# A graph network's node stages: the turn of the rows one pipeline step earlier, and another order of copies, roots and transfers

## Chip, cores and metric
The kernel runs on one core of one Trainium2 chip, in one launch. The metric is device time in microseconds (us), from the first to the last instruction with what lies around it. TensorE, VectorE, ScalarE, GpSimd and SyncE are called PE, DVE, ACT, POOL and SP in the profile. Each works through its own list of instructions in order; semaphores make one wait for another.

## What is computed
A two-layer graph transformer on 6250 nodes with 128 features and 100,000 edges, all in float32. Of the reference, what the node stages compute:

```python
h = relu(layernorm(x))                                  # first node stage
for l in range(2):
    k, q, v = (typed_linear(emb, ntype, W[l]) for W in (Wk, Wq, Wv))   # weights by node type (8)
    # per edge: k and v of the source go through a 16x16 matrix per head (8) and relation (8)
    # softmax over the edges of a target node, weighted sum of v: agg
    out = silu(typed_linear(agg, ntype, Wa[l]))
    al = sigmoid(skip[l][ntype])[:, None]
    out = out * al + emb * (1.0 - al)
    emb = (out - mean(out)) / sqrt(var(out) + 1e-5) * g[l] + b[l]
return x + emb @ Wff + bff
```

## The kernel before
Preparation (sort, lists, tables) fills the first 200 us or so. Then node stage 0, edge stage 0, node stage 1, edge stage 1 and node stage 2 follow one another. Each edge stage waits for the node stage ahead of it, and each node stage for the edge stage ahead.

All three node stages are the function `node_stage` with `l` = 0, 1 or 2; `first` is stage 0 and `last` is stage 2. The nodes are sorted by type into `TT` = 56 tiles of 128 rows, so that a tile has one type and one weight matrix; a type's last tile is mostly empty, and rows that stand for no node are not written.

One tile goes through these steps. (1) In stages 1 and 2, GpSimd gathers the sums of the edges (`n_ag`, L1113), TensorE turns them (L1035), ScalarE copies them out (`n_ag_t`, L952), TensorE multiplies by `Wa` (L1042), ScalarE applies silu (L958), and VectorE mixes with the old rows `h` (L838, L843). (2) VectorE takes mean and variance (L852, L856); for each group of four tiles VectorE adds epsilon (L861), ScalarE takes the root (`root`, L963) and VectorE the inverse (L866). Sqrt and silu need different activation tables, so an ACT_TABLE_LOAD stands before each change. (3) The norm is written to `n_norm`, by ScalarE in stage 0 (L970) and by VectorE later (L878). SP stores it to `node_h`. (4) TensorE turns the rows (`turn_rows`, L1048), and ScalarE copies them to `n_ht` (`rows_turned`, L977 or L979). (5) TensorE projects keys, values and queries into one PSUM bank (`project`, L1057 to L1059). ScalarE copies keys and values to `n_kv_t` (L994) and queries to `n_q_sb` (L997). (6) TensorE applies the eight relations (`relate`, L1074, 16 matmuls) into the four banks of `wide`. ScalarE copies two of them to `n_kv` (L987), VectorE the other two (L886). (7) GpSimd writes the tile's queries to `node_q` (`put_q`, L1118) and 8 KB per row to the table `node_kv` (`put_kv`, L1124). Stage 2 has `finish` (L1082) and `put_out` (L1130) instead of (5) to (7).

The order of the work is written by hand: `over(step)` calls each engine's `step(i)` for i from -9 on, and `real(i + n)` says which tile an operation handles in that step. The offsets set how far each operation runs ahead. `n_kv`, `n_norm` and `n_q_sb` have three buffers, `n_ht` and `n_kv_t` two, the PSUM tiles `ps_turn`, `ps_out` and `wide` one.

## Time and profile before

| | |
|---|---|
| time, median of 3 runs (lowest to highest) | 2920.91 us (2910.41 to 2944.08) |
| profiled execution: time, span | 2920.96 us, 2919.2 us |
| mean granted TensorE clock | 0.775 |
| busy: PE, DVE, ACT, POOL | 1917.2 (66%), 2112.4 (72%), 1775.0 (61%), 1967.6 (67%) us |
| DMA mean rate | 182 GB/s |
| node stage 0, table puts | 211.5 to 409.7 us |
| node stage 1, table puts | 1478.9 to 1703.9 us |
| node stage 2, gathers and output | 2742.0 to 2917.7 us |

Busy time is counted in which an engine executes; a wait for a semaphore is not busy. The granted clock is given as a share of 2.4 GHz, so 0.5 is 1.2 GHz. In a timeline row "idle before" is the time its engine stood still, with what ended it. A releaser called "issue" is time in which the engine waited for nothing that the profile shows.

### The profile page before, as it was taken

The page shows a single profiled execution, that of the slowest core. Times are in us where ns is not written, and L with a number is a line of the kernel's source. Part 1 is how long each engine was busy: PE and PEld are TensorE (multiplying, and loading weights), DVE is VectorE, ACT ScalarE, POOL GpSimd, SP SyncE. Part 2 cuts the span into 40 slices and gives each one's busy share as a digit, 9 for nine tenths or more (in the row PEclk, how much of TensorE's full clock was granted, in tenths as well). Part 3 has the DMA queues.
Part 4 walks back from the last instruction along what each step waited for, and adds up shares of the span by engine and source line. Part 5 has one row for each costly group of instructions (what it writes and reads, how often), then busy time and mean ns, then how long its engine had stood idle before and what let it go on. Part 6 is the DMA issues. An engine that isn't in the chain of part 4 may idle for free. (4 is left out here: it accounts for less than half of the span.)

```text
span 2919.2 us, 56192 instructions
## 1 busy us (share of the span) xinstructions
PE 1917.2 (66%) x12612; PEld 1649.1 (56%) x12612; DVE 2112.4 (72%) x5059; ACT 1775.0 (61%) x6725; POOL 1967.6 (67%) x2064
## 2 busy tenths in 40 slices
PE   1857746666666666666577747766766766766476
PEld 1745535666666666665455536666666665665344
DVE  7975547777777777777476757777777777777387
ACT  0015535667777766676666636677777677766455
POOL 3705567777777777777167667777777777776176
PEclk8558878887887888878688877778778788788555
DMA  5627776666666666666467676666666666665511
GB/s 138 93 70 296 293 270 199 185 185 188 181 183 184 184 185 186 184 182 182 110 225 273 261 228 188 185 185 182 183 185 185 185 188 182 183 185 144 159 44 36
DMA packets 427439, 530.01 MB, mean 182 GB/s; under 512 B 71241, under 2 KB 342155, under 8 KB 414612
## 3 DMA queue, kind: packets, MB, share of 16 engines
q0 software_dynamic: 102144, 327.28, 36.3%
q1 hardware_dynamic: 315864, 197.40, 23.5%
q10 hardware_dynamic: 9104, 1.86, 0.3%
q8 instruction: 97, 1.59, 0.2%
q14 instruction: 230, 1.88, 0.2%
HBM read 393.41 MB, written 150.71 MB: 186 GB/s over the span
## 5 line engine op out<-in xcount | busy, mean ns | idle before, releaser
L1268 POOL DMA_INDIRECT g_rows<-node_kv,g_ids x1568 | 1485.5, 947 | 475.8 <-issue 447.8
L1518 PE MATMUL g_ps_q<-g_qw,g_hot_t 128*128 128x128 f32 x3136 | 515.1, 320 | 249.8 <-DVE g_rows L1301 196.6
L1518 PEld LDWEIGHTS g_ps_q<-g_qw,g_hot_t 128*128 128x128 f32 x3136 | 462.4, 227 | 279.3 <-DVE g_rows L1301 220.5
L1438 ACT ACTIVATE acc<-acc,g_gained,g_scale x1568 | 606.1, 387 | 5.4 <-issue 3.6
L1301 DVE TENSOR_TENSOR g_rows<-g_rows,g_ps_q 128x512 f32<-128x512 f32 x448 | 275.9, 616 | 435.9 <-DMA g_rows<-node_kv,g_ids 401.3
L1499 PE MATMUL g_ps_sum<-g_hot,g_rows 128*128 128x128 f32 x3136 | 578.6, 342 | 9.5 <-ACT acc L1438 9.5
L1499 PEld LDWEIGHTS g_ps_sum<-g_hot,g_rows 128*128 128x128 f32 x3136 | 538.2, 256 | 12.1 <-ACT acc L1438 10.4
L1429 ACT ACTIVATE g_gained<-g_ps_sum,g_scale 128x1 f32<-128x1 f32 x1568 | 385.5, 246 | 111.4 <-PE g_ps_sum L1499 79.5
L1433 ACT ACTIVATE acc<-g_ps_sum 128x127 f32 x1568 | 416.1, 265 | 0.4
L1507 PE MATMUL g_ps_hot<-ident,g_hot_t 128*128 128x128 f32 x1568 | 313.6, 329 | 5.2 <-ACT g_hot L1443 4.9
L1456 ACT ACTIVATE g_exp_t<-g_shifted 112x128 f32<-112x128 f32 x112 | 34.7, 310 | 433.8 <-DVE g_shifted L1320 433.8
L1443 ACT ACTIVATE g_hot<-g_ps_hot 128x512 f32<-128x512 f32 x448 | 233.1, 521 | 54.6 <-PE g_ps_hot L1507 54.6
L1507 PEld LDWEIGHTS g_ps_hot<-ident,g_hot_t 128*128 128x128 f32 x1568 | 249.5, 178 | 6.5 <-ACT g_hot L1443 6.4
L1541 PE MATMUL g_ps_a<-g_ends,head_of_row 112*8 112x56 f32 x224 | 33.8, 242 | 332.3 <-DVE g_alpha L1335 332.3
L886 DVE COPY n_kv<-n_wide 128x512 f32<-128x512 f32 x224 | 148.6, 687 | 139.3 <-PE n_wide L1074 105.1
L1118 POOL DMA_INDIRECT node_q<-n_q_sb,node_slot x112 | 111.7, 997 | 188.2 <-ACT n_q_sb L997 169.0
L1289 DVE TENSOR_TENSOR g_hot_t<-g_rank_row,g_ps_a 128x1792 f32<-128x1792 bf16 x112 | 225.7, 2015 | 0.5 <-DMA g_rank_row<-edge_rank 0.4
L1374 DVE TENSOR_TENSOR g_rows<-g_rows,g_ps_b 128x1792 f32<-128x1792 f32 x112 | 224.8, 2007 | 0.0
L1113 POOL DMA_INDIRECT n_ag<-node_agg,node_slot x112 | 116.3, 1039 | 160.9 <-DMA node_agg<-n_agg 105.9
L1305 DVE TENSOR_REDUCE g_score<-g_rows 128x112 f32<-128x1792 f32 x112 | 224.0, 2000 | 0.1
L1541 PEld LDWEIGHTS g_ps_a<-g_ends,head_of_row 112*8 112x8 f32 x224 | 13.5, 87 | 359.4 <-issue 359.4
L1074 PE MATMUL n_wide<-bd,n_kv_t 32*128 32x256 f32 x1792 | 150.7, 457 | 73.2 <-ACT n_kv_t L994 67.8
(248 smaller groups left out, 3204.1 us busy)
## 6 DMA issues: line engine op xcount, KB each, us to landing
g_qw<-node_q SPq DMA_DIRECT2D x1568, 64.0 KB
g_rank_row<-edge_rank SPq DMA_DIRECT2D x114, 448.0 KB, 5.0
g_rows<-node_kv,g_ids POOLq DMA_INDIRECT x1568
node_h<-n_norm SPq DMA_DIRECT2D x112, 64.0 KB
n_h<-node_h SPq DMA_DIRECT2D x14, 512.0 KB, 6.9
node_agg<-n_agg SPq DMA_DIRECT2D x24, 256.0 KB, 2.9
node_rows<-node_x SPq DMA_DIRECT2D x2, 1792.0 KB
node_q<-l_blank_q SPq DMA_DIRECT2D x1, 3200.0 KB
```

What stands on the lines that cost most here:

```text
L1268: g_.indirect_dma_start(out=rows[j][:, g, :], out_offset=None, in_=scratch["kv"][:, :], in_offset=bass.IndirectOffsetOnAxis(ap=ids[half][: ...
L1289: v.tensor_tensor(hot_t[u][:, :, :].rearrange("p g e -> p (g e)"), rank_row[u][:, :], number_ps.to_broadcast([P, G * P]), ALU.is_equal).th ...
L1301: v.tensor_tensor(half, half, ps_q[k % 2][:, 0:len(four), :], ALU.mult).then_inc(s["prod"], 1)
L1305: v.reduce_sum(score[:, :, :], rows[j][:, :, 0:D].rearrange("p g (h d) -> p g h d", h=H), axis=AX.X).then_inc(s["score"], 1)
L1374: v.tensor_tensor(half, half, alpha_ps.rearrange("p (g h o) -> p g h o", h=H, o=1).to_broadcast([P, G, H, HS]), ALU.mult).then_inc(s["mess ...
L1429: a.activation(gained[g % 2][:, :], ps_sum[k % 2][:, g % FOUR, 0:1], ACT.Copy, scale=scale[j % 2][:, 1, g:g + 1]).then_inc(s["gained"], 1)
L1433: a.activation(acc[:, bass.ds(w + 1, P - 1)], ps_sum[k % 2][:, g % FOUR, 1:P], ACT.Copy).then_inc(s["copied"], 1)
L1438: a.activation(at, at, ACT.Identity, scale=scale[j % 2][:, 0, g:g + 1], bias=gained[g % 2][:, :]).then_inc(s["joined"], 1)
L1443: a.activation(hot[j][:, four[0]:four[-1] + 1, :], ps_hot[k % 2][:, 0:len(four), :], ACT.Copy).then_inc(s["turned"], 1)
L1499: ins = t.matmul(ps_sum[k % 2][:, g % FOUR, :], rows[j][:, g, D:2 * D], hot[j][:, g, :], start=True, stop=True)
L1507: ins = t.transpose(ps_hot[k % 2][:, n, :], hot_t[j % 2][:, g, :], c["ident"][:, :])
L1518: ins = t.matmul(ps_q[k % 2][:, n, :], hot_t[j % 2][:, g, :], qw[j % 2][:, g, :], start=True, stop=True)
```

## The change
The pipeline gets one more step (`over` starts at -10). Statistics, norm, turned rows and the first linear map each run one tile further ahead of the relations. Within a step the orders differ: TensorE projects directly behind the relations and turns rows for the tile after; ScalarE does its two `n_kv` copies and `n_kv_t` first, then queries, turned rows, root, norm, silu; VectorE puts its two copies together and norms behind them; GpSimd issues the table put ahead of the query put. The queries' copy has its own function, `queries_out`, whose wait for a free buffer stands behind `n_kv_t`. In stage 1 the registers with the tile types are loaded once for both users. The core of the diff:

```diff
         def over(step):
-            for i in range(-9, TT):
+            for i in range(-10, TT):
                 step(i)
...
                 def step(i):
-                    if real(i + 2) and not last:
-                        n = i + 2
+                    if real(i + 3) and not last:
+                        n = i + 3
                         sp.wait_ge(s["norm"], n + 1)
...
+                    if real(i + 10) and not first:
+                        linear_of(i + 10)
                     if real(i + 2) and not last:
                         weights_of(i + 2)
...
+                    if real(i + 8) and not first:
+                        gate(i + 8)
+                    if last and real(i + 1):
+                        biased(i + 1)
                     if real(i) and not last:
                         rows_out(i, 2)
...
                         rows_out(i, 3)
-                    if real(i + 7):
-                        statistics(i + 7)
+                    if real(i + 8) and not first:
+                        mix(i + 8)
+                    if real(i + 3) and (i + 3) % 4 == 0:
+                        inverses((i + 3) // 4)
+                    if real(i + 3) and not first:
+                        normalise(i + 3)
+                    if real(i + 8):
+                        statistics(i + 8)
...
+
+                def queries_out(i):
                     if i >= NQ:
                         act.wait_ge(q_put[i % NQ], count(q_put, i, i // NQ))
+                    act.wait_ge(s["qkv"], i + 1)
                     a.activation(q_sb[i % NQ][:, :], ps_out[:, 2 * P:3 * P], ACT.Copy).then_inc(s["q_sb"], 1)
 
                 def step(i):
-                    if real(i + 3) and (i + 3) % 4 == 0:
-                        root((i + 3) // 4)
-                    if real(i + 2) and first:
-                        normed(i + 2)
-                    if real(i + 1):
-                        rows_turned(i + 1)
                     if real(i) and not last:
                         rows_out(i, 0)
-                    if real(i + 8) and not first:
-                        silu(i + 8)
-                    if real(i) and not last:
                         rows_out(i, 1)
                     if real(i + 1) and not last:
                         projected(i + 1)
+                        queries_out(i + 1)
+                    if real(i + 2):
+                        rows_turned(i + 2)
+                    if real(i + 4) and (i + 4) % 4 == 0:
+                        root((i + 4) // 4)
+                    if real(i + 3) and first:
+                        normed(i + 3)
                     if real(i + 9) and not first:
-                        sums_turned(i + 9)
+                        silu(i + 9)
+                    if real(i + 10) and not first:
+                        sums_turned(i + 10)
...
                     if real(i) and not last:
                         relate(i)
                     if real(i + 1):
-                        turn_rows(i + 1)
-                    if real(i + 8) and not first:
-                        linear(i + 8)
-                    if real(i + 1):
                         if last:
                             finish(i + 1)
                         else:
                             project(i + 1)
                     if real(i + 9) and not first:
-                        turn_sums(i + 9)
+                        linear(i + 9)
+                    if real(i + 2):
+                        turn_rows(i + 2)
+                    if real(i + 10) and not first:
+                        turn_sums(i + 10)
...
-                    if real(i + 8 + AG) and not first:
-                        gather(i + 8 + AG)
-                    if real(i + 1) and not last:
-                        put_q(i + 1)
+                    if real(i + 9 + AG) and not first:
+                        gather(i + 9 + AG)
                     if real(i):
                         if last:
                             put_out(i)
                         else:
                             put_kv(i)
+                    if real(i + 1) and not last:
+                        put_q(i + 1)
```

TensorE in the middle of node stage 0, with the buffers' numbers. Before, one tile:

```order
L1074 MATMUL n0_wide<-bd0_0,n0_kv_t1 128x256 x4
L1074 MATMUL n0_wide<-bd0_1,n0_kv_t1 128x256 x4
L1048 MATMUL n0_ps_turn<-ident,n0_norm1 128x128
L1057 MATMUL n0_ps_out<-n0_ht0,n0_w_of1 128x128
L1058 MATMUL n0_ps_out<-n0_ht0,n0_w_of1 128x128
L1059 MATMUL n0_ps_out<-n0_w_of1,n0_ht0 128x128
```

After, the same relations and the same projection:

```order
L1080 MATMUL n0_wide<-bd0_0,n0_kv_t1 128x256 x4
L1080 MATMUL n0_wide<-bd0_1,n0_kv_t1 128x256 x4
L1063 MATMUL n0_ps_out<-n0_ht0,n0_w_of1 128x128
L1064 MATMUL n0_ps_out<-n0_ht0,n0_w_of1 128x128
L1065 MATMUL n0_ps_out<-n0_w_of1,n0_ht0 128x128
L1054 MATMUL n0_ps_turn<-ident,n0_norm2 128x128
```

The turn (`n0_ps_turn`) has moved behind the projection and handles the next tile's norm, `n0_norm2` for `n0_norm1`.

ScalarE in the middle of node stage 1, a step with a root. Before:

```order
L963 ACT_TABLE_LOAD
L963 ACTIVATE n1_var<-n1_var 128x4
L979 ACTIVATE n1_ht0<-n1_ps_turn,shift0,gain0 128x128
L987 ACTIVATE n1_kv1<-n1_wide 128x2x8x32
L958 ACT_TABLE_LOAD
L958 ACTIVATE n1_act_out1<-n1_ps_lin 128x128
L987 ACTIVATE n1_kv1<-n1_wide 128x2x8x32
L994 ACTIVATE n1_kv_t0<-n1_ps_out 128x256
L997 ACTIVATE n1_q_sb2<-n1_ps_out 128x128
L952 ACTIVATE n1_ag_t0<-n1_ps_ag 128x128
```

After:

```order
L990 ACTIVATE n1_kv1<-n1_wide 128x2x8x32 x2
L997 ACTIVATE n1_kv_t1<-n1_ps_out 128x256
L1003 ACTIVATE n1_q_sb2<-n1_ps_out 128x128
L982 ACTIVATE n1_ht0<-n1_ps_turn,shift0,gain0 128x128
L966 ACT_TABLE_LOAD
L966 ACTIVATE n1_var<-n1_var 128x4
L961 ACT_TABLE_LOAD
L961 ACTIVATE n1_act_out1<-n1_ps_lin 128x128
L955 ACTIVATE n1_ag_t0<-n1_ps_ag 128x128
```

The copies of `n1_wide` and of `n1_ps_out` have moved ahead of the root and the silu with their table loads.

GpSimd in the middle of node stage 0. Before:

```order
L1118 DMA node_q<-n0_q_sb1,node_slot 6400x128
L1124 DMA node_kv<-n0_kv0,node_id 6250x2048
L1118 DMA node_q<-n0_q_sb2,node_slot 6400x128
L1124 DMA node_kv<-n0_kv1,node_id 6250x2048
L1118 DMA node_q<-n0_q_sb0,node_slot 6400x128
```

After:

```order
L1130 DMA node_kv<-n0_kv0,node_id 6250x2048
L1124 DMA node_q<-n0_q_sb1,node_slot 6400x128
L1130 DMA node_kv<-n0_kv1,node_id 6250x2048
L1124 DMA node_q<-n0_q_sb2,node_slot 6400x128
L1130 DMA node_kv<-n0_kv2,node_id 6250x2048
```

The table put of a tile (`n0_kv0`) now stands ahead of the query put of the next tile (`n0_q_sb1`).

## Rows read from the trace of the kernel before
**Rows 1.** Windows: length; PE, PEld, DVE, ACT, POOL busy; clock, DMA share, GB/s.
```profile
211.50:409.70 198.20, 144.99 (x1241) 99.30 (x1241) 113.05 (x296) 120.50 (x336) 107.00 (x110) 0.87 0.75 293
1478.90:1661.20 182.30, 134.51 (x1125) 94.93 (x1125) 129.21 (x409) 126.52 (x335) 132.19 (x130) 0.87 0.73 275
1661.20:1703.90 42.70, 29.30 (x254) 20.33 (x254) 24.73 (x65) 26.68 (x66) 22.71 (x24) 0.86 0.62 242
2776.80:2894.10 117.30, 86.02 (x261) 56.86 (x259) 98.93 (x455) 69.06 (x162) 88.37 (x87) 0.50 0.15 44
...
217.00:236.00 19.00, 13.46 (x134) 9.13 (x126) 11.63 (x30) 12.44 (x34) 11.77 (x12) 1.00 0.84 324
236.00:262.00 26.00, 21.27 (x131) 14.49 (x131) 12.07 (x35) 12.23 (x36) 10.56 (x11) 0.54 0.67 263
...
392.00:395.00 3.00, 2.16 (x24) 1.43 (x23) 1.38 (x4) 2.00 (x7) 1.96 (x2) 1.00 0.97 385
```
**Rows 2.** Timeline, stage 0, clock 1.0: start, length, instruction, [idle before it].
```profile
378.93 0.49 PE L1057 MATMUL n_ps_out<-n_ht,n_w_of 128*128 128x128 f32 x2 [0.37 <-ACT n_ht L977]
...
379.90 0.38 ACT L994 ACTIVATE n_kv_t<-n_ps_out 128x256 f32<-128x256 f32 x1
...
380.34 1.15 PE L1074 MATMUL n_wide<-bd,n_kv_t 32*128 32x256 f32 x16 [0.47 <-ACT n_kv_t L994]
...
381.42 0.33 PE L1048 MATMUL n_ps_turn<-ident,n_norm 128*128 128x128 f32 x1
381.55 1.29 DVE L886 COPY n_kv<-n_wide 128x512 f32<-128x512 f32 x2 [1.08 <-PE n_wide L1074]
...
381.95 1.08 ACT L987 ACTIVATE n_kv<-n_wide 128x512 f32<-128x512 f32 x2
382.11 0.49 PE L1057 MATMUL n_ps_out<-n_ht,n_w_of 128*128 128x128 f32 x2 [0.37 <-ACT n_ht L977]
```
**Rows 3.** Timeline, stage 0, clock 0.5.
```profile
250.38 2.09 PE L1074 MATMUL n_wide<-bd,n_kv_t 32*128 32x256 f32 x16 [0.47 <-ACT n_kv_t L994]
...
253.25 0.79 PE L1057 MATMUL n_ps_out<-n_ht,n_w_of 128*128 128x128 f32 x2 [0.37 <-ACT n_ht L977]
...
254.93 0.38 ACT L994 ACTIVATE n_kv_t<-n_ps_out 128x256 f32<-128x256 f32 x1 [0.76 <-PE n_ps_out L1059]
...
255.37 2.09 PE L1074 MATMUL n_wide<-bd,n_kv_t 32*128 32x256 f32 x16 [0.47 <-ACT n_kv_t L994]
```
**Rows 4.** Waits, 205 to 411: who <- for whom: us, times, longest.
```profile
DVE n_kv L886 <- DMA node_kv<-n_kv,node_id: 21.5, 14, 2.8
```
**Rows 5.** Timeline, stage 0: two table puts and copies near them.
```profile
215.43 0.98 POOL L1124 DMA_INDIRECT node_kv<-n_kv,node_id  x1 [0.30 <-issue]
...
217.63 1.29 DVE L886 COPY n_kv<-n_wide 128x512 f32<-128x512 f32 x2 [1.02 <-PE n_wide L1074]
...
221.54 1.29 DVE L886 COPY n_kv<-n_wide 128x512 f32<-128x512 f32 x2 [1.76 <-DMA node_kv<-n_kv,node_id]
...
221.80 0.98 POOL L1124 DMA_INDIRECT node_kv<-n_kv,node_id  x1 [0.30 <-issue]
```
**Rows 6.** Groups on GpSimd, 1478 to 1662: busy, mean ns, idle, releasers.
```profile
L1113 POOL DMA_INDIRECT n_ag<-node_agg,node_slot x43 | 46.0, 1070 | 13.1 <-issue 10.1 <-ACT n_q_sb L997 2.7 <-DVE n_kv L886 0.3
L1118 POOL DMA_INDIRECT node_q<-n_q_sb,node_slot x44 | 44.8, 1018 | 25.4 <-issue 15.4 <-ACT n_q_sb L997 6.8 <-ACT n_kv L987 3.0
L1124 POOL DMA_INDIRECT node_kv<-n_kv,node_id x44 | 43.4, 985 | 13.4 <-issue 12.8 <-ACT n_kv L987 0.3 <-ACT n_q_sb L997 0.3
```
**Rows 7.** Timeline, stage 1: the relate after ScalarE's table loads.
```profile
1616.40 1.15 PE L1074 MATMUL n_wide<-bd,n_kv_t 32*128 32x256 f32 x16 [1.80 <-ACT n_kv_t L994]
```
**Rows 8.** Timeline of TensorE, stage 1, clock 0.5.
```profile
1600.10 0.48 PE L1048 MATMUL n_ps_turn<-ident,n_norm 128*128 128x128 f32 x1
...
1603.24 2.09 PE L1074 MATMUL n_wide<-bd,n_kv_t 32*128 32x256 f32 x16 [0.26 <-ACT n_kv_t L994]
1605.26 0.47 PE L1048 MATMUL n_ps_turn<-ident,n_norm 128*128 128x128 f32 x1
```

More of the change, by code:

```diff
@@ L777, in _ @@
                 v = nc.vector
-                regs = {n: [dve.alloc_register(f"dve_{n}{l}_{k}") for k in range(4)] for n in ("kind", "kind_a")}
+                regs = [[dve.alloc_register(f"dve_kind{l}_{u}{k}") for k in range(4)] for u in range(3)]
                 if not first:
@@ L802, in _, with kind @@
                                     ALU.mult).then_inc(s["built"], 1)
-                def kind(i, of):
-                    if i % 4 == 0:
-                        dve.reg_load(regs[of], tab["tile_type"][0:1, i:i + 4])
-                    return dve.snap(regs[of][i % 4], min_val=0, max_val=TN - 1)
+                def kind(i, ahead):
+                    four = regs[i // 4 % 3]
+                    if ahead and i % 4 == 0:
+                        dve.reg_load(four, tab["tile_type"][0:1, i:i + 4])
+                    return dve.snap(four[i % 4], min_val=0, max_val=TN - 1)
                 def weights_of(i):
-                    k = kind(i, "kind")
+                    k = kind(i, first)
                     if i == 0:
@@ L817, in linear_of @@
                 def linear_of(i):
-                    k = kind(i, "kind_a")
+                    k = kind(i, True)
                     if i == 0:
@@ L903, in step @@
                 def step(i):
[L904 to L907 removed]
+                    if real(i + 10) and not first:
+                        linear_of(i + 10)
                     if real(i + 2) and not last:
                         weights_of(i + 2)
[L910 to L915 removed]
+                    if last and real(i + 9):
+                        residual(i + 9)
+                    if real(i + 8) and not first:
+                        gate(i + 8)
+                    if last and real(i + 1):
+                        biased(i + 1)
                     if real(i) and not last:
                         rows_out(i, 2)
[L918 to L925 removed]
+                        rows_out(i, 3)
+                    if real(i + 8) and not first:
[6 more added lines that the diff above has]
+                        statistics(i + 8)
                     if last and real(i):
                         result(i)
[L928 to L931 removed]
+                    if real(i + 8):
+                        moments(i + 8)
+                        if (i + 8) % 4 == 3:
+                            variances((i + 8) // 4)
                 over(step)
@@ L994, in projected @@
                     a.activation(kv_t[i % 2][:, :, :], pairs(ps_out), ACT.Copy).then_inc(s["kv_t"], 1)
+                def queries_out(i):
                     if i >= NQ:
                         act.wait_ge(q_put[i % NQ], count(q_put, i, i // NQ))
+                    act.wait_ge(s["qkv"], i + 1)
                     a.activation(q_sb[i % NQ][:, :], ps_out[:, 2 * P:3 * P], ACT.Copy).then_inc(s["q_sb"], 1)
                 def step(i):
-                    if real(i + 3) and (i + 3) % 4 == 0:
-                        root((i + 3) // 4)
-                    if real(i + 2) and first:
-                        normed(i + 2)
-                    if real(i + 1):
-                        rows_turned(i + 1)
                     if real(i) and not last:
                         rows_out(i, 0)
-                    if real(i + 8) and not first:
-                        silu(i + 8)
-                    if real(i) and not last:
                         rows_out(i, 1)
```

18 lines of the change are left out of this document (removed).

## The prediction

> **What bounds the kernel now.** I read the page first: no engine is busy for more than 72% of the span, so the shares decide nothing and each stage has to be read alone. The diff touches the three node stages only. The edge stages, which hold most of the span, keep every instruction and order, so I let them cancel. Windows over the node stages [rows 1] give their length. Stage 0 from its first to its last table put (`node_kv`) takes 198.2 us for 55 steps, 3.60 each. Stage 1 takes 182.3 us for the first 43 steps (gathers still running), 4.24 each, and 42.7 us for the last 12, 3.56 each. Stage 2 takes 117.3 us for 43.5 pairs of GpSimd transfers, 2.70 each.
>
> The timeline of stage 0 shows one closed loop through TensorE and ScalarE [rows 2]. The relate (L1074) starts at 380.34, the turn of the next rows (L1048) at 381.42, then ScalarE copies the turned rows, and the projection starts at 382.11, 1.77 after the relate. A projection needs 0.97 until ScalarE's copy `kv_t` begins (378.93 to 379.90), and the next relate starts 0.44 after that. 1.77 + 0.97 + 0.44 = 3.18 us per tile. Each step waits for the one before it, on tile i+1 alone. At half clock the same loop is 250.38 to 255.37, 4.99 [rows 3].
>
> Two other things are close. The transfers: a full tile writes 128 rows of 8,192 + 512 + 512 bytes, 1.18 MB. The fullest windows run at 385 GB/s with a DMA share of 0.97 [rows 1], so a full tile cannot take under 3.06 us. VectorE already waits 21.5 us, 14 times, for a landed table put [rows 4]. And the ring of three `kv` buffers: copies of a tile start at 217.63, its put leaves at 221.80, because GpSimd first waits for the next tile's queries; a put of 215.43 frees its buffer at 221.54 [rows 5]. 4.17 + 6.11 = 10.28 over three buffers is 3.43 per tile when the transfers are full. The windows agree: stage 0 has clock 0.87, so 26% of 198.2 us, 52 us, ran at 0.5 (1.2 GHz), 10.3 tiles of 4.99. The other 44.7 tiles share 146.7 us, 3.28 each, between 3.18 and 3.43.
>
> In stage 1 GpSimd issues three transfers per tile: 1.070 + 1.018 + 0.985 us [rows 6], and 0.30 of issue before each, 3.97 us. Its idle in this stretch is 51.9 us; 131 transfers times 0.30 are 39.3 of it, so only 12.6 us is waiting. That is the most the stretch can give.
>
> **The change, part by part.** Nothing is added or removed in compute except 14 register loads on VectorE in stage 1. Everything else moves.
>
> *Turn and its copy leave the loop.* Now tile i+2 is turned behind the projection of i+1, and ScalarE copies it after the queries. What is left between two relates at clock 1.0: 1.21 until the copies of `wide` may start (380.34 to 381.55), 1.08 for ScalarE's two copies, 0.44 from `kv_t` to the relate, 2.73 us [rows 2]. The projection, now at once behind the relate, is done at 1.08 + 0.97 = 2.05, hidden under the copies. At 0.5: the relate's 2.09, then 1.68 from the projection's start to `kv_t` (253.25 to 254.93, now at once behind the relate), then 0.44: 4.21 us [rows 3]. The turn's 0.47 fits beside `kv_t`. Gain 0.78 per slow tile.
>
> *The table put moves ahead of the query put.* It leaves as the copies end, 1.35 after they start, not 4.17. The ring falls from 3.43 to (1.35 + 6.11) / 3 = 2.49. So neither loop nor ring binds at clock 1.0, and the next thing late is the transfers. A type has about 781 nodes: six full tiles and one of some 13 rows. Six at 3.06 and one at the loop's 2.73 make 3.01 per tile against 3.28. Behind the moved put stands the query put; its buffer is needed three tiles later, and `queries_out` now waits after `kv_t`, so no relate stands behind it. SP's store of `h` moves with the norm by one step; it keeps three buffers and three steps, as now, and costs nothing unless its landing exceeds three tiles.
>
> Stage 0: 44.7 x 3.01 + 10.3 x 4.21 = 177.9, a gain of 20.3 at an unchanged number of slow tiles. The bounds of the slow part: with none, 55 x 3.01 = 165.6, a gain of 32.6; with all, 55 x 4.21 = 231.6, a loss of 33.4. At 0.5 TensorE was busy 21.3 of 26 us and stayed there [rows 1]; after the change it is busy without a gap. I take a few fewer slow tiles, and 2.8 us for the earlier first put: 24 us.
>
> The clock fell after a wait for a table put: 0.84 DMA share at 1.0, then 0.54 clock in the next window [rows 1]. The Trainium skill, "TensorE: Matmul & The Clock Gate", section "HAM oscillation — how this bites in real kernels", says that waits for DMA between bursts of matmuls let the clock drop again and again; by it a kernel pushed against its transfers, as here, would sit at 1.2 GHz more, which is the second rival below. No row shows a stage that waits at each tile.
>
> *Roots and table loads.* In the tile with a root TensorE waited 1.80 us for `kv_t`, because the silu's load stood between the two table copies [rows 7]. Both loads now stand behind `kv_t` and the queries. Their number is the same. They still delay the next tile's copies, up to 2 us in one of four tiles; GpSimd's slack covers it, since the loop (2.73, with loads about 3.5 on average) stays under 3.97. Were that cover gone, a root would cost up to 2 us, 14 x 2 = 28.
>
> *Stage 1.* GpSimd still needs 3.97 for each tile with a gather, of which there are now 42 after the first put. The slow tile falls from 5.16 (1600.10 to 1605.26) to no less than 4.8, since TensorE idled only 0.26 and some 0.1 there [rows 8]; the ring's slack and the later query put absorb a spell. Bounds: 12.6 us gained if all waiting goes, 0 if none. I take 42 x 4.03 = 169. The last 13 tiles have two transfers, and are bound by the transfers or the loop, 3.01 to 4.2; I take 3.2 for them, 42. Together 211 against 225.0: 14 us. The extra step of fill costs a gather's 1.4, which the put that no longer waits for the second query gives back.
>
> *Stage 2* is bound by two transfers, 2 x (1.016 + 0.30) = 2.63 of its 2.70 [rows 1]. No gain there; one more step of fill (about 2) against one pair with a gather less and a looser tail: 0, between -3 and +3.
>
> **Sum.** 24 + 14 + 0 = 38 us. The profiled execution took 2920.96 (span 2919.2), the median is 2920.91, so the sum is made against both alike: 2883 us, 1.3% faster.
>
> **The rivals.** (1) *The clock stays up.* Gapless work at 0.5 brings it back within a tile: stage 0 gains 32.6 + 2.8, stage 1 18, stage 2 3: 2864. For it: TensorE would have no idle at 0.5 in stage 0. Against: 82% busy (21.27 of 26 us) did not bring it back, and the tables' waits stay. (2) *Waits for the transfers replace the loop's waits and pull the clock down more often.* With 20 slow tiles stage 0 takes 189.6, a gain of 8.6 and 2.8 for the first put; stage 1 gives 6: 2904. For it: the 14 waits [rows 4]. (3) *The transfers are already at their limit.* At 360 GB/s, between the 324 of the window at clock 1.0 and 385, a full tile takes 3.28, the average of seven 3.20. Stage 0 then gains 3.6 + 8 + 2.8, stage 1 10: 2897. The Trainium skill, "DMA: Bandwidth & Descriptors", section "Specifications", gives about 358 GB/s as a core's limit to HBM; by that estimate full tiles would be no faster than 3.30 us. The row of 385 GB/s speaks against a hard limit there. (4) *Slower.* The same clock mechanism as (2), carried through: from 27 slow tiles in stage 0 on (each costs 1.20 more) its gain is gone, with all 55 slow it loses 33, and stage 1 at 4.8 per tile loses another 0.56 x 43 = 24: 2978. Against it: more matmuls per us are done at 1.0 than before. (5) *No effect*: GpSimd and transfers hide all: 2919.
>
> **How the numbers follow.** Chances: forecast 0.50 (its own range 2871 to 2895), (1) 0.17, (2) 0.15, (3) 0.10, (4) 0.05, (5) 0.03. One per cent, 29 us, is about what a measurement of this kernel tells from no change; the line is 2892. Faster: 0.17 and 0.46 of the forecast's 0.50, 0.63. Same: 0.04 + 0.15 + 0.10 + 0.03 = 0.32. Slower: 0.05. The range 2862 to 2908 takes in (1), (2) and (3), and leaves out (4), (5) and a little at either end.
>
> **What would show it.** Right: relates 2.7 to 3.1 apart at clock 1.0 in stage 0, with VectorE's waits for table puts grown from 21.5 us; 4.2 at 0.5; the table put 1.4 after the copies start; a DMA share over 0.9 at clock 1.0; stage 1 at 3.95 to 4.05 per tile and its waits for `n_ps_turn` gone; stage 2 as long as now. Wrong: a stage 0 clock under 0.75, relates waiting for `kv_t` behind the table loads in stage 1, or a norm waiting for the store of `h`.

## The result
The changed kernel is slower: 2956.15 us (median, 2952.48 to 2956.68) against 2915.66 us for the kernel before in the same runs (2905.8 to 2944.08), a ratio of 1.0126 with a 95% interval of 1.0089 to 1.0163. The prediction was 2883 us, 1.3% faster.

The lengths of the stages in the profiled executions (stage 0 from its first to its last table put, stages 1 and 2 from their first gather to their last put or output):

| us | before | after | difference | forecast |
|---|---|---|---|---|
| up to the first table put | 211.5 | 209.1 | -2.4 | -2.8 |
| node stage 0 | 198.1 | 166.7 | -31.4 | -21.2 |
| edge stage 0 | 1041.7 | 1041.5 | -0.2 | 0 |
| node stage 1 | 252.5 | 234.8 | -17.7 | -14 |
| edge stage 1 | 1038.2 | 1038.9 | +0.7 | 0 |
| node stage 2 | 174.7 | 261.4 | **+86.7** | 0 |
| span | 2919.2 | 2954.9 | +35.7 | -38 |

Two stages gain more than was forecast, 49.1 us. The third, which was booked at nothing, gives back all of it and 37.6 us more.

Windows of after, to set beside [rows 1] (length; PE, PEld, DVE, ACT, POOL busy; clock, DMA share, GB/s):

```profile
209.00:375.80 166.80, 118.78 (x1257) 87.70 (x1257) 112.13 (x294) 114.51 (x338) 108.79 (x111) 0.97 0.91 348
240.00:260.00 20.00, 15.08 (x173) 11.16 (x165) 14.66 (x41) 14.45 (x44) 13.98 (x15) 1.00 0.96 369
1444.00:1610.00 166.00, 122.59 (x1103) 92.49 (x1096) 128.74 (x402) 124.73 (x329) 127.15 (x124) 0.89 0.77 288
2728.00:2912.00 184.00, 66.03 (x246) 50.75 (x245) 93.89 (x429) 64.12 (x156) 85.93 (x82) 0.50 0.09 27
```

Stage 0 now runs at clock 0.97 instead of 0.87, with the transfers at 348 GB/s for the whole stage (before: 293) and at 369 in the 20 us from 240 on. Stage 2 has fallen from 44 to 27 GB/s, and all engines in it are less busy: in 184 us VectorE works 93.9 and GpSimd 85.9.

**Stage 0.** Timeline of after (some rows left out), one full tile at clock 1.0, to set beside [rows 2, 5]:

```profile
351.65 1.04 POOL L1130 DMA_INDIRECT node_kv<-n_kv,node_id  x1 [0.68 <-ACT n_q_sb L1003]
352.61 1.08 ACT L990 ACTIVATE n_kv<-n_wide 128x512 f32<-128x512 f32 x2 [1.02 <-DMA node_kv<-n_kv,node_id]
352.62 1.29 DVE L890 COPY n_kv<-n_wide 128x512 f32<-128x512 f32 x2 [0.78 <-DMA node_kv<-n_kv,node_id]
354.05 1.15 PE L1080 MATMUL n_wide<-bd,n_kv_t 32*128 32x256 f32 x16 [0.97 <-ACT n_kv_t L997]
354.74 0.98 POOL L1130 DMA_INDIRECT node_kv<-n_kv,node_id  x1 [0.76 <-ACT n_q_sb L1003]
```

In this tile both halves of the copy out of `wide` wait for a landed table put, no longer for TensorE. From put to put it takes 3.09 us (351.65 to 354.74). The table of waits over 203 to 376 adds them up. In the kernel before VectorE had 21.5 us in 14 such waits [rows 4] and ScalarE 5.5 us in 8, so the growth is all on ScalarE; about half of the 56 tiles wait:

```profile
ACT n_kv L990 <- DMA node_kv<-n_kv,node_id: 28.5, 27, 2.4
DVE n_kv L890 <- DMA node_kv<-n_kv,node_id: 21.1, 21, 2.8
```

**Stage 1.** GpSimd's groups over 1444 to 1610, to set beside [rows 6] (busy, mean ns | idle before, releasers):

```profile
L1119 POOL DMA_INDIRECT n_ag<-node_agg,node_slot x41 | 43.2, 1054 | 12.5 <-issue 11.9 <-DVE n_kv L890 0.6
L1130 POOL DMA_INDIRECT node_kv<-n_kv,node_id x42 | 43.1, 1027 | 14.8 <-issue 11.0 <-ACT n_q_sb L1003 2.5 <-DVE n_kv L890 1.2
L1124 POOL DMA_INDIRECT node_q<-n_q_sb,node_slot x41 | 40.9, 997 | 12.5 <-issue 12.5
```

Nearly all its idle time is now "issue": 35.4 of 39.8 us; before it was 38.3 of 51.9.

**Stage 2.** The table of waits of the kernel before, over 2777 to 2917, shows what the prediction had not read:

```profile
POOL out_nodes L1130 <- issue: 17.6, 46, 0.8
PE n_ps_out L1082 <- DVE n_y L896: 9.7, 24, 0.8
```

TensorE's `finish` already waited 24 times for VectorE's `result` (`n_y`), 0.4 us each, while GpSimd's waits for its outputs were mostly issue (for `n_y` it waited 9.5 us, in 7 tiles). The same waits of after, over 2728 to 2912:

```profile
ACT n_ht L982 <- PE n_ps_turn L1054: 121.4, 41, 4.6
PE n_ps_out L1088 <- DVE n_y L900: 116.8, 41, 5.3
DVE n_act_out L842 <- ACT n_act_out L961: 83.6, 41, 4.4
POOL out_nodes L1136 <- DVE n_y L900: 64.8, 37, 4.2
```

One tile of stage 2 in after (rows left out at "..."). Its instructions on three engines form a ring, in which each starts only behind the one before it:

```profile
2844.35 0.28 DVE L900 TENSOR_TENSOR n_y<-n_ps_out,n_xr 128x128 f32<-128x128 f32 x1
...
2844.77 0.77 PE L1088 MATMUL n_ps_out<-n_wff,n_ht 128*128 128x128 f32 x2 [2.04 <-DVE n_y L900]
2845.33 0.63 PE L1048 MATMUL n_ps_lin<-n_wa,n_ag_t 128*128 128x128 f32 x2
2845.76 0.42 PE L1054 MATMUL n_ps_turn<-ident,n_norm 128*128 128x128 f32 x1
2846.22 0.46 ACT L982 ACTIVATE n_ht<-n_ps_turn,shift,gain 128x128 f32<-128x128 f32 x1 [2.86 <-PE n_ps_turn L1054]
2846.57 0.27 ACT L961 ACTIVATE n_act_out<-n_ps_lin 128x128 f32<-128x128 f32 x1
2846.87 0.29 DVE L842 TENSOR_TENSOR n_act_out<-n_act_out,n_h 128x128 f32<-128x128 f32 x1 [1.44 <-ACT n_act_out L961]
...
2848.01 0.27 DVE L900 TENSOR_TENSOR n_y<-n_ps_out,n_xr 128x128 f32<-128x128 f32 x1
```

The steps, from start to start: `result(i)` frees the one `ps_out` buffer; `finish(i+1)` (L1088) had waited 2.04 us for it. Behind `finish` in TensorE's order stand `linear(i+9)` (L1048) and the turn (L1054). ScalarE copies `n_ht` and only then does the silu of `linear`; VectorE had waited 1.44 us for the silu with `gate(i+9)` (L842), and `result(i+1)` stands at the end of VectorE's step, behind that gate. 0.42 + 0.56 + 0.43 + 0.46 + 0.35 + 0.30 + 1.14 = 3.66 us per tile. In the tile with a root both table loads lie in the ring:

```profile
2834.32 0.77 PE L1088 MATMUL n_ps_out<-n_wff,n_ht 128*128 128x128 f32 x2 [2.03 <-DVE n_y L900]
2836.24 1.28 ACT L966 ACT_TABLE_LOAD   x1
2837.53 0.20 ACT L966 ACTIVATE n_var<-n_var 128x4 f32<-128x4 f32 x1
2837.75 1.28 ACT L961 ACT_TABLE_LOAD   x1
2839.05 0.28 ACT L961 ACTIVATE n_act_out<-n_ps_lin 128x128 f32<-128x128 f32 x1
...
2841.12 0.76 PE L1088 MATMUL n_ps_out<-n_wff,n_ht 128*128 128x128 f32 x2 [5.18 <-DVE n_y L900]
```

From `finish` to `finish` 6.80 us. Three of 3.66 and one of 6.80 are 4.44 on average, and the first 43 outputs are 4.47 apart; before they were 2.73 apart. The 3.14 us more are the two loads (1.28 each) and the root (0.20) with what lies between. On this the Trainium skill, "ScalarE: Activation LUTs", section "What ACT_TABLE_LOAD costs", gives about 1283 ns for a load and a drain of about 1380 ns with it. The load agrees; no drain shows here, since the copy of `n_ht` (2835.76, 0.46 long) ends at 2836.22, the load starts at 2836.24, and the root follows the load's end at once.

In the kernel before the same ring spans two tiles. Its rows (others between them left out):

```profile
2827.70 0.27 DVE L896 TENSOR_TENSOR n_y<-n_ps_out,n_xr 128x128 f32<-128x128 f32 x1
2828.12 0.77 PE L1082 MATMUL n_ps_out<-n_wff,n_ht 128*128 128x128 f32 x2 [0.32 <-DVE n_y L896]
...
2829.47 0.79 PE L1042 MATMUL n_ps_lin<-n_wa,n_ag_t 128*128 128x128 f32 x2 [0.15 <-ACT n_ag_t L952]
...
2830.30 0.28 ACT L958 ACTIVATE n_act_out<-n_ps_lin 128x128 f32<-128x128 f32 x1 [0.49 <-PE n_ps_lin L1042]
...
2831.27 0.28 DVE L838 TENSOR_TENSOR n_act_out<-n_act_out,n_h 128x128 f32<-128x128 f32 x1
...
2832.26 0.27 DVE L896 TENSOR_TENSOR n_y<-n_ps_out,n_xr 128x128 f32<-128x128 f32 x1
```

From `result(i-1)` over `finish(i)`, `linear(i+8)`, its silu and its gate to `result(i+1)` it takes 4.56 us, and `result(i)` lies between (2829.86). That is 2.28 us per tile, hidden behind GpSimd's 2.63.

Which edge was moved does not show in the order within a step, only in the tile numbers. TensorE's step had `linear(i+8)` ahead of `finish(i+1)` and now has `linear(i+9)` behind it. In both kernels that puts `linear` of tile n+8 between `finish` of n and `finish` of n+1. The copy of the turned rows of tile n also stands ahead of the silu of n+7 in both. VectorE's order is another: ahead of `result(i)` stood `gate(i+7)`, and now stands `gate(i+8)`. That gate needs the `linear` that stands behind `finish(i)`. So `result(i)`, which frees the next `finish`, waits for everything behind the last one, and the tile of slack is gone.

### The profile page after: what moved, and what is told of

It is laid out like the page before. It is cut to its first block and busy times, and to the rows that moved or that the text cites. A ratio compares the mean times of both kernels' runs of the same rounds, so it can differ in the third digit from the quotient of the medians.

```text
span 2954.9 us, 56284 instructions
## 1 busy us (share of the span) xinstructions
PE 1848.6 (63%) x12612; PEld 1621.5 (55%) x12612; DVE 2112.8 (72%) x5059; ACT 1764.4 (60%) x6725; POOL 1969.5 (67%) x2064
## 5 line engine op out<-in xcount | busy, mean ns | idle before, releaser
L1524 PEld LDWEIGHTS g_ps_q<-g_qw,g_hot_t 128*128 128x128 f32 x3136 | 456.2, 225 | 287.1 <-DVE g_rows L1307 228.2
L1080 PE MATMUL n_wide<-bd,n_kv_t 32*128 32x256 f32 x1792 | 139.6, 427 | 82.3 <-ACT n_kv_t L997 52.5
L990 ACT ACTIVATE n_kv<-n_wide 128x512 f32<-128x512 f32 x224 | 121.7, 596 | 100.0 <-DMA node_kv<-n_kv,node_id 52.6
```

What stands on the lines that cost most here:

```text
L1524: ins = t.matmul(ps_q[k % 2][:, n, :], hot_t[j % 2][:, g, :], qw[j % 2][:, g, :], start=True, stop=True)
```

## The experiments
**The chips differ.** The runs came in five groups, each on one chip. In three (the result's among them) an edge stage takes 1038 to 1044 us and the kernel before 2916 to 2926 in the median. In the other two an edge stage takes 1277 to 1299 us and the kernel before 3498 and 3557; these are called slow chips below, the others quick ones. Stages are only compared on chips of one kind.

**The changed kernel again,** unchanged, on a quick chip.

> The changed kernel itself, for its stage lengths on this chip. Theory A: stage 2 is 75 to 90 us longer than that of result_first_b and the other stages within 5 us of it.

Measured: 2961.64 us; stages 168.1, 234.0 and 261.2, each within 1.4 us of the first execution.

**VectorE's `result` first.** If the ring is the cause, it opens where `result(i)` no longer stands behind `gate(i+8)`; it still stands behind `gate(i+7)`, as in the kernel before:

```diff
                 def step(i):
+                    if last and real(i):
+                        result(i)
                     if real(i + 10) and not first:
                         linear_of(i + 10)
...
-                    if last and real(i):
-                        result(i)
```

> The changed kernel with one line moved: in stage 2 VectorE makes y(i) at the head of its step, ahead of the gate that waits for the silu. Theory A: y(i) no longer stands behind the silu, the loop is cut, and stage 2 falls to the pace of GpSimd's two transfers, 2.65 to 2.8 us per tile against 4.2 now; stage 2 in 172 to 182 us, the time 2865 to 2880. Rival C (the two table loads that now stand together behind the turned rows on ScalarE set the pace, 5.5 us in one tile of four): the tiles with a root stay at 5 us or more, stage 2 above 200 us, the time above 2895.

It was measured on a slow chip: 3524.79 us against 3498.07, ratio 1.0104 (1.0027 to 1.018), but stage 2 took 192.6 us. Again, on a quick chip:

> The kernel of result_first once more, since the chip of the first comparison moved memory slower (its edge stages took 1280 us each, against 1040), and the transfers hid the gain of stages 0 and 1 there. Theory A: where edge stages take 1040 us, stage 0 is 30 to 35 us and stage 1 15 to 18 us shorter than before, stage 2 within 5 us of before; time 2865 to 2880. Rival B (the gain of the first two stages needs the slower stage 2, or was this one execution's luck with the clock): the time stays above 2895.

Measured: 2891.41 us against 2922.61, ratio 0.9877 (0.9825 to 0.993). Stage 2 took 192.4 us instead of 261.4. Moving one instruction of VectorE gave back 69 of the 86.7 us, so the ring was the cause of these. Neither expectation had the size: stage 2 is 17.7 us longer than before, not within 5, and the tiles with a root take less than 5 us. Ordinary tiles were 2.65 to 2.70 us apart, GpSimd's pace; every fourth was 4.16. The timeline of this kernel shows such a tile:

```profile
2781.85 1.28 ACT L966 ACT_TABLE_LOAD   x1
2783.36 1.28 ACT L961 ACT_TABLE_LOAD   x1
2784.66 0.28 ACT L961 ACTIVATE n_act_out<-n_ps_lin 128x128 f32<-128x128 f32 x1
2784.83 0.27 ACT L955 ACTIVATE n_ag_t<-n_ps_ag 128x128 f32<-128x128 f32 x1
2785.16 0.80 PE L1048 MATMUL n_ps_lin<-n_wa,n_ag_t 128*128 128x128 f32 x2 [2.23 <-ACT n_ag_t L955]
```

The two loads still stand back to back in front of the silu and of the copy of the turned sums (`n_ag_t`, L955), for which TensorE's `linear` waits 2.23 us.

**`linear` ahead of `finish` on TensorE,** in the new pipeline, stage 2 only:

```diff
+                    if last and real(i + 9):
+                        linear(i + 9)
                     if real(i + 1):
                         if last:
                             finish(i + 1)
...
-                    if real(i + 9) and not first:
+                    if real(i + 9) and not first and not last:
                         linear(i + 9)
```

> The changed kernel with TensorE's linear map for i+9 put ahead of the last matmul for i+1 in stage 2. Theory A: only the linear map's 0.6 us leaves the loop, since the silu still stands behind the turned rows on ScalarE, and their turn behind the last matmul: an ordinary tile goes from 3.66 to about 3.1 us, stage 2 from 262 to 225 to 240, the time about 2925. Theory A' (the linear map alone is what closes the loop): stage 2 falls to 180 us or less, the time to 2875 or less.

Measured, on a slow chip: stage 2 241.5 us, 4.04 per tile in the mean and 3.23 in an ordinary one (time 3557.24); the changed kernel was not measured there. The 3.1 that was expected for the smaller ring is near; the stage is a little over the 225 to 240. The ring closes again through its next member: the turn stands behind `finish`, and ScalarE's silu behind the copy of the turned rows. It is not enough to take `linear` from behind the waiting instruction: ScalarE must not wait for anything behind it either before it does the silu.

**The kernel before with `finish` ahead of `linear`,** stage 2 only. It puts `linear` of tile n+7 behind `finish` of n, where it stood ahead. So the slack of one tile goes here too, but on TensorE instead of VectorE:

```diff
+                    if last and real(i + 1):
+                        finish(i + 1)
                     if real(i + 8) and not first:
                         linear(i + 8)
-                    if real(i + 1):
-                        if last:
-                            finish(i + 1)
-                        else:
-                            project(i + 1)
+                    if real(i + 1) and not last:
+                        project(i + 1)
```

> The kernel of before with one order changed in stage 2 alone: TensorE does the last matmul for i+1 ahead of the linear map for i+8. Theory A: the same loop closes without ScalarE's part (the silu does not stand behind turned rows that wait for the last matmul): y, last matmul, linear map, silu, gate, y: 0.4 + 0.8 + 0.6 + 0.3 + 0.3 + 0.9 = 3.0 to 3.3 us per tile against 2.70, stage 2 10 to 35 us longer, the time 2930 to 2950. Rival C (ScalarE's table loads behind the turned rows are what costs): this order costs nothing, time 2915 to 2921.

On a slow chip stage 2 took 196.3 us (time 3524.08), with nothing of before beside it. Again:

> The kernel before; in stage 2 alone TensorE's `finish(i + 1)` moves ahead of `linear(i + 8)`. Measured again on the quicker chip. Theory A (the harm is that `linear`, and all that hangs on it, stands behind `finish`, which waits for the last instruction of VectorE's step): stage 2 is longer than 174.7 us even in the old pipeline, about 182 to 200, since here the turned rows of the tile still stand ahead and `gate` of the same step is two tiles behind; the time is 2926 to 2946. Rival (only the deeper pipeline is at fault): 173 to 177 and 2910 to 2922.

This was a slow chip too: 195.8 us (3541.23). Once more, with the kernel before on the same chip:

> The kernel before with TensorE's `finish(i + 1)` ahead of `linear(i + 8)` in stage 2. On the slower chip its puts were 2.96 us apart, 3.66 with a root. If that is the loop through `finish`, stage 2 is 15 to 22 us longer than before_again's beside it, on either chip (about 193 to 197 on the quicker one, time 2932 to 2942); if only the deeper pipeline harms, it is within 3 us of it.

Measured: 2946.66 us, stage 2 195.8 us, against 174.5 of the kernel before on the same chip; puts 2.96 us apart, 3.66 with a root. Its table of waits, over 2800 to 2920:

```profile
ACT n_act_out L958 <- PE n_ps_lin L1042: 62.2, 30, 2.1
PE n_ps_out L1082 <- DVE n_y L896: 40.2, 30, 1.3
```

TensorE's wait for `n_y` rises from 9.7 us (in 140 us) to 40.2 (in 120). This is one execution, but the two on slow chips have the same stage 2. A ring over one tile costs the old pipeline 21 us. It is shorter than that of the changed kernel (2.96 per tile against 3.66), because the turn and ScalarE's copy are not in it. It does not clear the extra step: in the changed kernel it was that step, `gate` one tile further ahead, that closed the ring. A version with only `gate` moved in the old pipeline was not run.

**Before's order in stage 2,** the rest as changed. VectorE, ScalarE and TensorE call before's `step` where `last` is true, and the new one elsewhere; GpSimd keeps the new one:

```diff
                 def step(i):
+                    if last:
+                        ...
+                    else:
                     ...
```

> The changed kernel, but in node stage 2 VectorE, ScalarE and TensorE keep the order of before. Theory A (all of the loss is one closed loop in stage 2: sum y(i) on VectorE, then the last matmul for i+1, the linear map for i+9 behind it, the turn, ScalarE's turned rows and silu behind those, the gate, and VectorE's work up to y(i+1)): stage 2, from its first gather to its last output transfer, goes from 262 us back to 174 to 178, the time to about 2869 (2862 to 2876). Rival B (stage 2 became slower by its surroundings, a colder start or the edge stage before it, and not by its order): stage 2 stays above 240 us and the time above 2930.

On a slow chip: 3508.46 us, ratio 1.0031 (1.0005 to 1.0057), stage 2 188.6. Again:

> The changed kernel, but VectorE, ScalarE and TensorE keep the order of before in stage 2; measured again on a chip whose edge stages take 1040 us, since the first run of it fell on a slower one. Theory A (what stage 2 lost is its order alone): stage 2 takes 174 to 178 us at 2.73 per tile, and the time is 2955 minus 261.4 plus 176, about 2870 (2866 to 2876). Rival (the gathers that run a step further ahead cost stage 2 something too, as the 2.99 per tile on the slower chip could mean): stage 2 takes 186 to 190, the time is 2880 to 2885.

On the other slow chip: 3557.51 us, ratio 0.9986 (0.9961 to 1.0011), stage 2 189.5. On a quick chip:

> The changed kernel with before's order on VectorE, ScalarE and TensorE in stage 2. On the quicker chip: if the order is all, stage 2 takes 174 to 178 and the time is 2866 to 2876; if the gathers, a step further ahead, cost something, 186 to 190 and 2880 to 2886. On the slower chip: as before_again within 2 us by the first, 10 to 15 longer by the second.

Measured: 2868.88 us against 2925.88, ratio 0.9806 (0.9783 to 0.9829), stages 166.2, 235.0 and 175.8. With the order of before, stage 2 is within 1.3 us of before (174.5), and the whole kernel is 1.9% faster. The rival, that the deeper gathers cost something, falls for quick chips; on the slow ones the kernel before was not profiled unchanged.

**`result` first, and the root at the end of ScalarE's step.** The last 17.7 us were put down to the two loads in a row:

```diff
                     if real(i + 2):
                         rows_turned(i + 2)
-                    if real(i + 4) and (i + 4) % 4 == 0:
+                    if real(i + 4) and (i + 4) % 4 == 0 and not last:
                         root((i + 4) // 4)
...
                     if real(i + 10) and not first:
                         sums_turned(i + 10)
+                    if real(i + 4) and (i + 4) % 4 == 0 and last:
+                        root((i + 4) // 4)
```

> The version with `result` first, and in stage 2 alone ScalarE's `root` moves from between `rows_turned` and `silu` to the end of the step, behind `sums_turned`. So the load for the root and the load for the silu are no longer back to back: the copy of the next turned rows stands between them, and the silu and the turned sums of the root's own step no longer wait for either. Theory L (the 4.17 us of every fourth tile are two loads in a row in front of the silu, each 1.28, of which one can be hidden): tiles with a root fall from 4.17 to about 2.9 to 3.2, stage 2 takes 175 to 181 us instead of 192.4, and the time is 2874 to 2881, against 2891.4 with `result` first alone. Rival (ScalarE's load stands on the path wherever it is, or the deeper pipeline itself costs it): stage 2 stays at 190 to 194, the time at 2889 to 2893.

On a slow chip: 3552.35 us against 3557.16, ratio 0.9981 (0.9955 to 1.0007), stage 2 189.6. On the quick chip:

> `result` first, and in stage 2 ScalarE's `root` at the end of its step. On the quicker chip: if two table loads in a row ahead of the silu are the 17.7 us, stage 2 takes 175 to 181 and the time is 2874 to 2881; if the load is on the path wherever it stands, stage 2 takes 190 to 194 and the time is 2889 to 2893. On the slower chip it took 189.6 against 192.2 to 192.6 with `result` first alone, so there only 3 us came back; the trace showed tiles of 4.2 to 4.5 us at every fourth to fifth place, which speaks for the second.

Measured: **2865.53 us** against 2925.88, ratio 0.9793 (0.977 to 0.9817), stages 166.6, 235.6 and 171.0. This is the best version. Only 3 us had come back on the slow chip; here 21.4 did, more than the first theory's 11 to 17, and stage 2 is 3.5 us shorter than in the kernel before. Its timeline at a root (start, length, [idle before]) and its window of stage 2:

```profile
2780.36 1.28 ACT L966 ACT_TABLE_LOAD   x1
2781.66 0.20 ACT L966 ACTIVATE n_var<-n_var 128x4 f32<-128x4 f32 x1
2781.83 0.46 ACT L982 ACTIVATE n_ht<-n_ps_turn,shift,gain 128x128 f32<-128x128 f32 x1
2782.31 1.28 ACT L961 ACT_TABLE_LOAD   x1
2782.78 1.02 POOL L1121 DMA_INDIRECT n_ag<-node_agg,node_slot  x1 [0.31 <-issue]
2784.11 1.05 POOL L1138 DMA_INDIRECT out_nodes<-n_y,node_id  x1 [0.31 <-issue]
...
2727.00:2862.00 135.00, 86.96 (x302) 63.20 (x301) 114.95 (x516) 75.62 (x185) 99.81 (x97) 0.50 0.14 43
```

The first load now runs while TensorE does `finish`, `linear` and the turn, where ScalarE waited for the turn anyway; the second follows the copy. GpSimd issues 1.02 and 1.05 us with 0.31 between them, without a wait, also at the root. The outputs are 2.66 us apart in the mean, GpSimd's bound.

**The order of the two puts.** Twice, once on the kernel before (the table put first) and once on the version with `result` first (the query put first again, the reverse of this diff):

```diff
-                    if real(i + 1) and not last:
-                        put_q(i + 1)
                     if real(i):
                         if last:
                             put_out(i)
                         else:
                             put_kv(i)
+                    if real(i + 1) and not last:
+                        put_q(i + 1)
```

> The kernel of before with one edit: GpSimd issues the table put ahead of the next tile's query put. Theory D (the ring of three buffers held stage 0 back as much as the loop): the ring falls from 3.4 to 2.5 us per tile and only the loop of 3.18 is left; stage 0 is 5 to 8 us shorter, stage 1 0 to 3. Rival E (the put order is most of the gain, since the put leaves 2.8 us earlier): stage 0 is 20 us or more shorter. Rival F (the put order is worth nothing alone): within 2 us.

> The kernel of result_first, but GpSimd issues the next tile's query put ahead of the table put, as before. Theory D: the queries now come 1.8 us after the copies start, later than the copies' end by 0.5, so the put leaves 3.1 us after them and not 1.35: ring (3.1 + 6.1) / 3 = 3.07 per tile against transfers of 3.01; stage 0 is 0 to 8 us longer than in result_first_b, stage 1 0 to 5. Rival E: stage 0 gives back 15 us or more.

Measured: the first took 2910.69 us with 188.9 in stage 0 and 253.9 in stage 1. But stage 0 of the unchanged order took 198.1, 187.0 and 203.0 us in three profiled executions on quick chips (clock 0.87, 0.94 and 0.84), so the length alone shows nothing. An estimate takes the clock out as the prediction did: a clock of 0.90 means 37.8 us, 7.6 tiles of 4.99, at half clock, and leaves 3.19 us for each other tile. The same sum gives 3.28, 3.26 and 3.29 for the unchanged order. So the put order alone is worth some 0.1 us per tile, and leaves the loop's 3.18, as expected.

The second took 2910.78 us: stage 0 181.8, stage 1 238.4, against 167.7 and 234.6. Stage 0 of the new order took between 166.2 and 168.1 in five profiled executions, so 14 us lie outside that spread. The waits of both engines for landed puts are 68.5 us against 47.5. By the same estimate (slow tiles of 4.21) the other tiles take 3.13 us against 2.96, which is some 8 us; the rest is a lower clock, 0.90 against 0.95. So the ring over three buffers held stage 0 back where the put was late. How much of the gain that is, this one execution doesn't say well: about half of stage 0's gain is left in it (181.8 against a mean of 196.0 for before's order and 167.1 for the new one), and neither expectation, 0 to 8 us or 15 and more, had the 14.

**The kernel before again,** as the measure for the last group.

> The kernel before, unchanged, for its own stage lengths on this chip. On a chip whose edge stages take 1040 us: stage 0 about 198, stage 1 252, stage 2 175 us. On one with 1290 us for an edge stage: if the slower memory is why the two orders take 189.5 us in stage 2 there, this one takes 186 to 192 as well; if the changed order is why, it takes 174 to 178.

Measured: 2907.41 us, stages 187.0, 250.1 and 174.5, clock 0.94 in stage 0; that stage was expected 11 us longer.

**Four `n_kv` buffers:**

```diff
-    KV, NQ, AG = 3, 3, 4
+    KV, NQ, AG = 4, 3, 4
```

> The version with `result` first, with four `n_kv` buffers instead of three. Stage 0 there takes 167.7 us (3.05 per tile) with waits of VectorE and ScalarE for landed table puts (28.5 and 21.1 us in the changed kernel). Theory T (these waits are the transfers at their limit): a fourth buffer changes nothing that lasts, stage 0 stays at 164 to 168 us. Rival (the ring of three buffers still binds): stage 0 falls to 150 to 160 us, the loop's 2.73 per tile, and the time to 2876 to 2885.

It was measured on a slow chip, 3562.11 us, stage 0 207.5 us, no shorter than the 207.0 and 208.7 with three buffers beside it. There the DMA share of the stage is 0.72, against 0.91 in after, so this run does not test the transfers as the limit. For the quick chips it stays open whether a fourth buffer would help.

## Why the prediction was wrong
**Stage 2, the step that failed.** "*Stage 2* is bound by two transfers, 2 x (1.016 + 0.30) = 2.63 of its 2.70 [rows 1]. No gain there" priced only what already bound the stage, and booked 0, between -3 and +3, where 86.7 us were lost. It used a bound from below as a forecast. It never asked what `result` waits for once `gate(i+8)` stands ahead of it; the orders were followed for stages 0 and 1 only. The sum could have been begun from the trace of before. It has 0.42 us from `result` to `finish`, 0.56 from there to the next matmul, 0.46 from the turn to its copy, 0.31 from the silu to the gate (2834.76 to 2835.07) and 1.00 from the gate to `result`. These five terms make 2.75, already above 2.70; the whole ring measured 3.66, and 6.80 with a root. With 43 tiles at 4.47 instead of 2.73 this is 75 us, and the last 12 pairs (9.3) and 2.5 us of fill make the rest of 86.7. None of the rivals named it: the slower one, 2978, was near in size, and its mechanism did not happen.

**Stage 0: right in kind, too small.** The loop was forecast at 2.73 us per tile; where the transfers don't hold it back (the first tiles of after) the puts are 2.64 apart. "The next thing late is the transfers" held: 49.6 us in 48 waits for landed puts on two engines (before: 27.0 in 22), 3.09 from put to put against 3.06. VectorE's own waits, which were named as the sign, did not grow (21.1 against 21.5). The ring over three buffers was mis-sized: the put leaves 2.13 us after the copies start (352.61 to 354.74), not 1.35, and the put of 345.41 frees its buffer 7.20 us later, not 6.11. So (2.13 + 7.20) / 3 = 3.11 where the forecast had 2.49; the landing is longer while the transfers are full (DMA share 0.99 from 320 to 340).

What was mis-sized most is the number of slow tiles: somewhat under 10.3 at 4.21 were forecast. The clock was 0.97, so only 6% of the stage, 10 us or two to three tiles, ran at 0.5. Rival (1) had this, in size and in mechanism, "Gapless work at 0.5 brings it back within a tile". Windows of after show it (length, PE busy, ..., clock, DMA share, GB/s):

```profile
231.00:233.00 2.00, 0.45 (x8) 0.48 (x12) 1.83 (x5) 1.89 (x7) 0.73 (x1) 0.98 1.05 429
233.00:235.00 2.00, 2.00 (x18) 1.35 (x12) 0.84 (x3) 0.91 (x3) 1.46 (x2) 0.50 0.67 250
237.00:239.00 2.00, 1.49 (x19) 0.92 (x11) 1.30 (x3) 1.45 (x6) 1.61 (x2) 1.00 0.81 311
```

TensorE was busy for all of 233 to 235 and the clock was back by 237. In the kernel before TensorE was busy 82% of the time at 0.5, and its slow spells lasted 24 us (238 to 262 and 296 to 320). Rival (1) gave stage 0 and the first put 32.6 + 2.8 = 35.4 against a measured 31.4 + 2.4 = 33.8. Part of that is the base, since 198.1 was one of the longer lengths of before (187.0 to 203.0).

**The clock rivals (2) and (4): half their mechanism, not their outcome.** They said that waits for transfers would pull the clock down more often. It did fall in the middle of stage 0 after TensorE's long waits for its table copy, 1.71 us ahead of 232.55 and 2.16 ahead of 263.44, but it came back within some 4 us each time. The waits of the other tiles up to 370, at most 1.32 us, did not lower it, and over the stage it rose from 0.87 to 0.97. The long spells of the kernel before had followed waits of 1.31 and 1.46 us (ahead of 236.53 and 294.55), so the length of the one wait does not tell the two kernels apart. What differs is how busy TensorE was at 0.5. The Trainium skill, "TensorE: Matmul & The Clock Gate", section "HAM oscillation — how this bites in real kernels", describes a kernel whose wait for data behind each burst of matmuls is longer than the burst. The prediction applied it to any kernel that waits for transfers. Here most waits are shorter than the 2.1 us of matmuls in a tile, so this stage is not its case, and no run here shows one.

**Rival (3), transfers at 360 GB/s: wrong in its number.** The window from 240 on moved 369 GB/s over 20 us. The Trainium skill's figure of about 358 GB/s for a core ("DMA: Bandwidth & Descriptors", section "Specifications") is passed there as well, by 3%.

**Stage 1: right.** 225.0 us from first to last table put were to become 211; they became 208.1. GpSimd's idle time is nearly all issue, as forecast, and ScalarE's waits for `n_ps_turn` are gone. The gap at a root has moved as forecast too: VectorE waits up to 3.0 us for the silu (13 waits, 24.2 us), while GpSimd's waits for other engines come to 4.3 us (1444 to 1610).

**What is left without the failing step** is 2954.9 - 86.7 = 2868 us. The two versions that repair stage 2 measured 2868.88 and 2865.53. The forecast of 2883 was for this kernel, and 15 us too high.

## What to carry to other kernels
Where a change reorders in-order queues that stages share, read every stage that runs them, also one in which nothing is to be gained. Compare the orders by tile numbers and not by places in a step: two instructions that change places, one of them a tile further ahead, may keep their order, and two that keep their places may lose it. For each instruction that comes to stand behind another, ask what that other waits for, and add up the ring of waits from its rows. A stage's present bound says only how fast it can't be; the forecast is the larger of it and each ring, and one move can bring a ring from two tiles down to one. Put an instruction that frees a single buffer as early in its engine's step as its inputs allow, and a table load where its engine would wait anyway.

## What the hardware showed
The gain hung on the chip. On the slow chips the gathers of the edge stages wait far longer. GpSimd's group over 500 to 1700 of the best version on a slow chip, and over 400 to 1400 on a quick one:

```profile
L1276 POOL DMA_INDIRECT g_rows<-node_kv,g_ids x758 | 719.3, 949 | 443.8 <-issue 197.6 <-PE g_ps_sum L1507 131.1 <-remote 114.6
```

```profile
L1276 POOL DMA_INDIRECT g_rows<-node_kv,g_ids x769 | 728.3, 947 | 232.3 <-issue 219.1 <-PE g_ps_sum L1507 11.0 <-POOL g_ids L1266 2.3
```

The same transfers are issued in the same 949 and 947 ns, but on the slow chip, in 1200 us, there are 131.1 us of waits for TensorE (11.0 on the quick one, in 1000), and 114.6 us whose releaser the trace calls "remote", which no quick chip shows. In stage 2 there ScalarE's copy of the turned rows waits 22.8 us in 6 such waits:

```profile
ACT n_ht L982 <- remote: 22.8, 6, 5.2
```

Stage 0 of the new order takes 202 to 209 us on these chips, and on them before's order took 189.8 and 210.1. So no gain of stage 0 shows there. The outputs of the best version are 3.03 us apart instead of 2.66, and the ratios of the two repaired versions are 0.9981 to 1.0031 instead of 0.98. What "remote" stands for, and why these chips have it, no run here settles; that their memory is slower, as some of the expectations put it, is not shown.
